# A conditioned transformer block on one core: a new start for the first tile, and new orders of work on every engine

## The reference

```python
def _tc_rmsnorm(x, t, gw, gb, bw, bb):
    g = (t @ gw.T + gb)[:, None, :]
    b = (t @ bw.T + bb)[:, None, :]
    inv_rms = jax.lax.rsqrt(jnp.mean(x * x, axis=-1, keepdims=True) + EPS)
    return g * x * inv_rms + b

x1 = x + _attention(_tc_rmsnorm(x, t, g1w, g1b, b1w, b1b), Wq, Wk, Wv, Wo)   # 16 heads of 16
block = x1 + _swiglu(_tc_rmsnorm(x1, t, g2w, g2b, b2w, b2b), gate_w, hid_w, out_w)   # hidden 1024
return x + block
```

## Time and profile before

| | |
|---|---|
| median of three runs (lowest, highest) | 959.45 us (959.16, 959.62) |
| the profiled execution: time, span on the core | 959.58 us, 957.5 us |
| busy: PE, PEld | 908.0 us (95%), 773.5 us (81%) |
| busy: DVE, ACT, POOL | 664.8 us (69%), 559.4 us (58%), 451.9 us (47%) |
| mean granted TensorE clock | 0.986 |
| chain that ended last | PE 82%, ACT 6%, issue 5%, DVE 3%, POOL 2% |

### The profile page before, as it was taken

The page is one execution under the profiler, slowest core; times in us unless marked ns, Lnnn a source line. Parts: engine busy times, 40 slices in busy tenths (PEclk is TensorE's granted clock), DMA queues, the critical chain, the costliest instruction groups (busy, mean ns, idle before and its releaser), DMA issues.

```text
span 957.5 us, 24194 instructions
## 1 busy us (share of the span) xinstructions
PE 908.0 (95%) x8988; PEld 773.5 (81%) x8988; DVE 664.8 (69%) x1082; ACT 559.4 (58%) x1255; POOL 451.9 (47%) x394
## 2 busy tenths in 40 slices
PE   5678999999999999999999999999999999999998
PEld 4466888878888887888888888888888888788887
DVE  3647768576875857778586877858687685868652
ACT  4556656656665666656566655655666566565542
POOL 4454525354463545436354543535455354544433
PEclk9779999999999999999999999999999999999999
DMA  5300101010110101011010111101010010200000
GB/s 191 98 26 23 34 25 56 1 55 22 44 33 22 39 16 55 22 44 33 7 47 22 44 32 44 33 0 55 22 44 33 23 53 0 55 0 1 24 23 23
DMA packets 25595, 34.06 MB, mean 36 GB/s; under 512 B 3296, under 2 KB 20896, under 8 KB 25440
## 3 DMA queue, kind: packets, MB, share of 16 engines
q1 hardware_dynamic: 25344, 33.59, 11.2%
q10 hardware_dynamic: 224, 0.10, 0.0%
HBM read 25.27 MB, written 8.42 MB: 35 GB/s over the span
## 4 chain that ended last, share of the span: by engine, by line
PE 82%; ACT 6%; issue 5%; DVE 3%; POOL 2%; DMA 1%; ACTq 1%; DVEq 0%; SPq 0%; POOLq 0%
PE ps L1082 8%; PE ps L1084 7%; PE ps L1083 7%; PE ps L1221 7%; PE ps L1237 6%; PE ps L1193 6%; PE ps L1227 6%; PE ps L1222 6%; PE ps L1240 6%; PE ps L1238 6%; PE ps L1183 4%; PE ps L1110 4%; PE ps L1208 4%; PE ps L1111 3%; PE ps L1113 3%
## 5 line engine op out<-in xcount | busy, mean ns | idle before, releaser
L284 POOL TENSOR_TENSOR h_lo<-h,h_hi 128x512 fp32r<-128x512 f32 x128 | 165.7, 1295 | 142.4 <-ACT h_hi L511 142.4
L290 POOL TENSOR_TENSOR probs<-probs,recip 128x512 f32<-128x512 f32 x128 | 134.5, 1058 | 105.6 <-DVE recip L825 105.5
L1082 PE MATMUL ps<-out_w_hi,h_hi 128*128 128x256 f32 x512 | 147.2, 287 | 0.7
L1084 PE MATMUL ps<-out_w_hi,h_lo 128*128 128x256 f32 x512 | 144.4, 282 | 0.0
L1083 PE MATMUL ps<-out_w_lo,h_hi 128*128 128x256 f32 x512 | 144.1, 281 | 0.0
L506 ACT ACTIVATE shared<-ps 128x512 f32<-128x512 f32 x128 | 76.1, 595 | 99.7 <-PE ps L1227 99.4
L836 DVE SCALAR_TENSOR_TENSOR shared<-shared,ps 128x512 f32<-128x512 f32 x128 | 87.4, 683 | 46.4 <-ACT shared L506 44.9
L516 ACT ACTIVATE probs<-probs 128x512 f32<-128x512 f32 x128 | 80.7, 631 | 62.5 <-DVE probs L813 61.9
L1221 PE MATMUL ps<-xn_hi,gate_w_hi 128*128 128x512 f32 x256 | 110.2, 430 | 0.4 <-DVE shared L836 0.2
L843 DVE SCALAR_TENSOR_TENSOR h<-shared,ps 128x512 f32<-128x512 f32 x128 | 87.4, 683 | 30.1 <-PE ps L1240 28.7
L1237 PE MATMUL ps<-xn_hi,hid_w_hi 128*128 128x512 f32 x256 | 105.1, 410 | 0.0
(11 more groups left out here) (92 smaller groups left out, 2016.6 us busy)
## 6 DMA issues: line engine op xcount, KB each, us to landing
x_in<-in_x SPq DMA_DIRECT2D x16, 512.0 KB, 3.4
xT_in<-in_xT SPq DMA_DIRECT2D x16, 512.0 KB, 3.2
out<-result SPq DMA_DIRECT2D x15, 512.0 KB, 3.0
inv_all<-inv_rows SPq DMA_DIRECT2D x15, 256.0 KB, 3.8
shared<-in_attT SPq DMA_DIRECT2D x1, 1024.0 KB, 7.8
shared<-in_gateT SPq DMA_DIRECT2D x1, 1024.0 KB, 9.7
shared<-in_hidT SPq DMA_DIRECT2D x1, 1024.0 KB, 5.0
shared<-in_outT SPq DMA_DIRECT2D x1, 1024.0 KB, 5.7
```

The source lines that it names most:

```text
L284: nc.gpsimd.tensor_tensor(h_lo[:, j % KEPT, :], h[:, j % 2, :], h_hi[:, j % KEPT, :].bitcast(F32), ALU.subtract).then_inc(h_lo_done, 1)
L290: nc.gpsimd.tensor_tensor(own, own, recip[:, p % TOGETHER, :].unsqueeze(2).to_broadcast([P, SEQS, L]), ALU.mult).then_inc(divided, 1)
L1082: nc.tensor.matmul(dst, a_hi, b_hi, start=first, stop=False, skip_group_check=skip)
L1084: return nc.tensor.matmul(dst, a_lo, b_hi, start=False, stop=last, skip_group_check=skip)
```

## The change

Semaphores of keys and queries are renamed for the half that they tell of (`keys0_done`, `keys1_done`, `queries0_done`, `queries1_done`), whichever engine makes it.

The start: TensorE spreads the factors ahead of both modulations. VectorE scales into two banks of PSUM, applies gain and shift to both halves there itself (`whole_norm1`) and leaves the result in `xn1`; ScalarE's `second_norm1(0)` goes. ScalarE rounds the weights of values and output after the norm, not before.

The first tile: the copies go crosswise. ScalarE copies both halves of the keys and the second queries, VectorE the first queries. The casts and low parts of gate, hid and out weights move to other places in the lists.

Other tiles: the scores wait for the values of both engines alone, and steps change places in `steady_tile`, `last_tile` and `after_last` on all four engines. No step of these is added or dropped.

```diff
@@ GpSimd
             def first_tile(t, ahead):
-                low_hid_weights()
+                low_gate_weights()
                 divide(t, 0)
+                next_inverse(t)
                 divide(t, 1)
-                next_inverse(t)
                 divide(t, 2)
...
                 divide(t, 7)
+                low_hid_weights()
                 low_norm1(t + 1, 0)
                 low_norm1(t + 1, 1)
                 low_out_weights()
@@ ScalarE
             squares1(0)
...
+            high_att_weights(0)
             for c in range(CH):
                 high_norm1(0, c)
-            high_weights(1, gate_w_in, 16, gate_w_hi[:, :, :].rearrange("p c n -> p (c n)"), 1)
-            first_keys(0)
-            first_queries(0)
+            high_att_weights(1)
...
             def first_tile(t, ahead):
+                high_gate_weights()
+                first_keys(t)
+                keep_input(t)
+                other_keys(t)
+                exp(t, 0)
+                other_queries(t)
+                exp(t, 1)
                 high_hid_weights()
-                keep_input(t)
                 first_values(0)
-                exp(t, 0)
-                exp(t, 1)
+                exp(t, 2)
+                keep_transposed(t, 0)
                 squares1(t + 1)
...
@@ VectorE
                 if alone(u):
                     dve.wait_ge(inv1_mm, 1)
                     factors = ps[:, PAIR, :].rearrange("p (k q) -> p k q", k=BLK)
+                    scaled = ps[:, PAIR + 2:PAIR + 4, :]
...
+            def whole_norm1():
+                for c in range(CH):
+                    scaled = ps[:, PAIR + 2 + c, :].rearrange("p (b q) -> p b q", q=L)
+                    last = nc.vector.tensor_tensor(scaled, scaled, of_sequences(0, c, 0), ALU.mult)
+                last.then_inc(gained1, 1)
+                dve.wait_ge(gained1, 1)
+                for c in range(CH):
+                    nc.vector.tensor_tensor(xn1[:, c, :].rearrange("p (b q) -> p b q", q=L),
+                                            ps[:, PAIR + 2 + c, :].rearrange("p (b q) -> p b q", q=L),
+                                            of_sequences(1, c, 0), ALU.add).then_inc((xn1_first, xn1_second)[c], 1)
...
             def first_tile(t, ahead):
+                first_queries(t)
                 row_maxima(t, 0)
-                second_keys(0)
                 row_maxima(t, 1)
+                row_maxima(t, 2)
                 shift(t, 0)
...
             def steady_tile(t, finish, ahead):
...
                 low_attention(t, 1)
                 second_queries(t + 1)
+                silu(u, 7)
+                hidden(u, 7)
                 first_residual(t)
+                second_keys(t + 1)
                 scale_second_rest(t)
                 first_norm2(t)
                 second_values(t + 1)
@@ TensorE
                 elif r == 0:
-                    pe.wait_ge(k_act_done, t + 1)
-                    pe.wait_ge(k_dve_done, t + 1)
-                    pe.wait_ge(q_act_done, t + 1)
-                    pe.wait_ge(q_dve_done, t + 1)
+                    pe.wait_ge(v_dve_done, t + 1)
                     pe.wait_ge(v_act_done, t + 1)
-                    pe.wait_ge(v_dve_done, t + 1)
-                    pe.wait_ge(x1_done, 2 * t)
...
+            pe.wait_ge(consts_in, 16)
+            spread_factors()
             pe.wait_ge(mod_in, 2 * 16)
             gains_and_shifts(0)
-            pe.wait_ge(consts_in, 16)
-            spread_factors()
             gains_and_shifts(1)
...
             def first_tile(t, ahead):
                 project_k(0, 1)
                 scores(t, 0)
+                project_v(0, 1)
                 project_q(0, 1)
-                project_v(0, 1)
                 project_v(0, 0)
+                transpose_probs(t, 0)
                 scores(t, 1)
-                transpose_probs(t, 0)
...
             def steady_tile(t, finish, ahead):
...
                 hid(u, 1)
+                transpose_probs(t, 0)
+                gate(u, 2)
                 down(u, 0)
-                gate(u, 2)
                 hid(u, 2)
-                transpose_probs(t, 0)
...
                 values_probs(t, 1)
                 project_q(t + 1, 1)
-                project_k(t + 1, 0)
+                hid(u, 7)
                 project_out(t, ahead)
-                down(u, 5)
-                hid(u, 7)
                 project_k(t + 1, 1)
                 project_v(t + 1, 1)
+                down(u, 5)
                 transpose_norm2(t, 0)
                 transpose_norm2(t, 1)
                 project_v(t + 1, 0)
```

More of the change, by code:

```diff
@@ L485, in first_keys @@
                                                 scale=head_mask[:, head:head + 1])
-                last.then_inc(k_act_done, 1)
+                last.then_inc(keys0_done, 1)
             def first_queries(u):
                 act.wait_ge(q_mm, CH * u + 1)
-                nc.scalar.copy(queries[:, 0, :], ps[:, q_bank(u, 0), :]).then_inc(q_act_done, 1)
+                nc.scalar.copy(queries[:, 0, :], ps[:, q_bank(u, 0), :]).then_inc(queries0_done, 1)
             def first_values(u):
@@ L934, in first_tile, with steady_tile, last_tile @@
                 scale_second_rest(t)
+                second_values(t + 1)
+                first_norm2(t)
+            def steady_tile(t, finish, ahead):
+                u = t - 1
+                low_norm2(u)
+                results(t - 2)
+                row_maxima(t, 0)
+                shift(t, 0)
+                silu(u, 0)
+                hidden(u, 0)
+                reciprocals(t, 0)
+                row_maxima(t, 1)
+                silu(u, 1)
+                shift(t, 1)
+                row_maxima(t, 2)
+                hidden(u, 1)
+                reciprocals(t, 1)
+                silu(u, 2)
+                row_maxima(t, 3)
+                shift(t, 2)
+                shift(t, 3)
+                hidden(u, 2)
+                reciprocals(t, 2)
+                silu(u, 3)
+                reciprocals(t, 3)
+                hidden(u, 3)
+                silu(u, 4)
+                hidden(u, 4)
+                row_maxima(t, 4)
+                row_maxima(t, 5)
+                shift(t, 4)
+                low_attention(t, 0)
+                shift(t, 5)
+                scale_rows(t + 1)
+                reciprocals(t, 4)
+                reciprocals(t, 5)
+                first_norm1(t + 1)
+                silu(u, 5)
+                row_maxima(t, 6)
+                hidden(u, 5)
+                shift(t, 6)
+                row_maxima(t, 7)
+                shift(t, 7)
+                reciprocals(t, 6)
+                reciprocals(t, 7)
+                silu(u, 6)
+                hidden(u, 6)
+                low_attention(t, 1)
+                second_queries(t + 1)
+                silu(u, 7)
+                hidden(u, 7)
+                first_residual(t)
+                second_keys(t + 1)
+                scale_second_rest(t)
                 first_norm2(t)
                 second_values(t + 1)
-            def steady_tile(t, finish, ahead):
+            def last_tile(t, finish, ahead):
                 u = t - 1
@@ L1372, in last_tile @@
                 hid(u, 1)
+                down(u, 0)
                 transpose_probs(t, 0)
@@ L1377, in last_tile @@
                 gate(u, 3)
-                hid(u, 3)
                 transpose_probs(t, 2)
                 transpose_probs(t, 3)
+                hid(u, 3)
+                scores(t, 1)
                 gate(u, 4)
-                scores(t, 1)
+                down(u, 1)
                 hid(u, 4)
-                down(u, 0)
-                down(u, 1)
-                gate(u, 5)
                 values_probs(t, 0)
                 transpose_probs(t, 4)
+                gate(u, 5)
                 down(u, 2)
+                transpose_probs(t, 5)
                 hid(u, 5)
                 gate(u, 6)
-                transpose_probs(t, 5)
                 transpose_probs(t, 6)
@@ L1396, in last_tile @@
                 values_probs(t, 1)
+                gate(u, 7)
+                project_out(t, ahead)
+                hid(u, 7)
                 down(u, 3)
-                project_out(t, ahead)
-                gate(u, 7)
-                hid(u, 7)
                 down(u, 4)
@@ L1424, in after_last @@
                 hid(u, 5, False)
+                down(u, 2)
                 gate(u, 6)
```

277 lines of the change are left out of this document (118 added, 159 removed).

## The result

The kernel after takes 954.69 us (median of five runs, 952.91 to 955.30) against 959.62 us before (five runs beside it): a ratio of 0.994, 95% interval 0.9924 to 0.9955. So it is faster by 4.9 us, about half a percent, where I forecast 14.9; the interval lies clear of 1. Its profiled execution took 954.4 us, with a span of 952.4 us (957.5 before).

| stretch | before | after | difference | forecast |
|---|---|---|---|---|
| start to scores of tile 1 | 79.64 | 73.53 | −6.1 | −6.5 |
| tile 1 | 57.45 | 58.20 | +0.75 | −0.3 |
| tiles 2 to 14, 13 x | 56.45 | 56.20 | −3.2 | −7.2 |
| scores of tile 15 to the end | 86.62 | 90.05 | +3.4 | −0.9 |

A forecast was written before the change was run, and what follows sets the result against it. TensorE was taken to bound the loop, a chain through all engines the first tile. First tile −6.5, tile 1 −0.3, thirteen loop tiles −7.2 and the end −0.9 make −14.9: from 959.58 to 944.7 us, range 938 to 955.

The forecast's parts named there:

- The first tile: From the start to the scores of tile 1: a shorter chain through all engines, −6.5 us (bounds −3 and −9).
- the rows speak for PSUM as the reason: Norm at the start: gain and shift out of PSUM take 0.65 us each, against 1.93 and 2.73 beside GpSimd.
- The faster products: Start: without TensorE's wait, products run at the higher clock sooner; 1.6 us taken back (bounds 0 and 2.4).
- the hidden weights' low part: First tile: moved behind divide 7 on GpSimd, 4.6 us ahead of xn1_lo; projections start at 53.7 to 54.5.
- The waits: Ahead of each tile's scores: seven waits become two, −0.27 us per tile.
- The orders of the loop: Loop tiles: new step orders give −0.28 us per tile, mostly from down 0 finding its low part ready.
- Elsewhere I find no product later than its inputs: Loop: apart from down 0 no product waits for inputs; tightest are transpose 0 (0.1 to 0.25 us ahead) and transpose 3.
- The end: Last tile: −0.6 us at the norm's transposes and −0.3 from waits, −0.9 us in all (bounds 0 and −1.3).
- The last part trades one early stall for another: nothing: The last part, at the kernel's end: one early stall replaces another, no change in time.
- Tile 1: The tile after the first, with a slow clock at its start in either kernel: −0.3 us.
- Rival (d): Tile's end: second keys' copy delays VectorE's scaling of the second residual, 1.2 us lost per tile; 966 us, chance 0.08.
- Rival (a): Loop: the orders give nothing and only the shorter wait works; 948.7 us, chance 0.17.

## Why the prediction was right and wrong

- **The first tile: right in sum, and partly for the wrong reason.** The scaling came at 9.13 (I said 9.1), two gains or two shifts took 1.3 (0.65 each), the scaling for tile 1 began at 42.98 (near 44), the projections of tile 1 began at 54.67 (53.7 to 54.5), the scores at 73.53 (73.1). But "the rows speak for PSUM as the reason" gave the place too much: it is worth 1.0 of 3.8 us. (My upper end, "20.1, that is as late as before", compared the norm's end with that of xn_lo; the norm ended at 18.11.) The faster products gave back 2.2 us where I took 1.6: from the projections to the first scores it takes 4.49 us (16.45 to 20.94) for 6.73 (20.23 to 26.96). And I priced the hidden weights' low part as a step in series on GpSimd. In fact VectorE's add was held until it ended, and the casts came behind that. The two ways happen to end at nearly the same time, so the number was right by luck; an earlier place takes 3.4 us off.
- **The waits: right.** −0.27 forecast, −0.22 measured alone. But the sum has one seam too many: of the fifteen, one stands in the first tile's 6.5 us, one in tile 1 and thirteen in the loop, and "−0.3 from the waits" in the last tile has none left.
- **The orders of the loop: the step that failed.** I took −0.28, as "the chain transposes, norm, casts, values is the same length". Its steps are the same, but not what runs beside them: the scaling took 1.0 us more beside a low part, and TensorE lost 0.73 us of it. I had the price before me, for I took just that for the late step in the last tile, and I didn't ask in the loop what GpSimd would do when its input came earlier. ScalarE's cast of chunk 7 moved ahead of the squares, and so GpSimd's low part became ready before the inverse behind which it was listed. The orders' own gain was mis-sized too: 0.76 us, not 0.28. I looked for idle time, "at most about 13 us in the loop", and found one late product, down 0. "Elsewhere I find no product later than its inputs" was wrong: a projection and a hid waited in each tile as well, in time that the profile counts as TensorE's busy time, out of which 9.4 us came.
- **VectorE beside GpSimd.** The Trainium skill, page "SBUF — State Buffer", section "Who interferes with whom", says that a VectorE instruction in a two-port mode, as `tensor_scalar` can be, contends with GpSimd, and one with two SBUF inputs with GpSimd's reads of SBUF, and that whichever starts first holds up the other for the whole of its instruction. The runs agree: two scalings took 0.61 us alone and 1.63 when GpSimd's 1.28 us began 0.07 us ahead; an add took 0.69 alone and 4.87 behind the start of 4.94.
- **The end: wrong.** −0.6 for the stall at the transposes was right, the stall is gone. For a new stall within the last tile I had no term; the nearest, "The last part trades one early stall for another: nothing", failed. The stall is 2.85 us of standing at the values' products, and the lower clock behind that. With the 0.69 us won at the transposes, the stretch still lost 3.4 us. I hadn't followed VectorE's new list in the last tile to the bank that hid and attention share.
- **Tile 1: wrong in sign.** I put in −0.3, with a slow clock "at its start in either kernel". It is at the lower level behind the scores of tile 1 until about 83 us before (granted clock 0.51 from 80 to 82, 0.64 from 82 to 84), some 3.4 us, and from 73.53 to about 78 after (0.50 from 74 to 78, 0.97 from 78 to 80), some 4.5, behind a stand of 4.73 us instead of 3.51; tile 1 took 0.75 us more. The run with filling products puts the clock's whole price in that tile at 2.1 us (57.67 to 55.59).
- **The rivals.** The measured time lies at the upper end of the range, and came by none of the rivals as written. Rival (d) named the place, the gap ahead of the norm's transposes, but its mechanism, the second keys, cost nothing. Rival (a) gave the right size for the loop: the orders came to nothing, but as a gain of 0.76 and a loss of 0.73 us per tile.

## What to carry to other kernels

When a step becomes ready earlier, look at what it then runs beside: here a cast that ScalarE made earlier moved a step of GpSimd onto one of VectorE's. Put GpSimd's long SBUF work where VectorE reads PSUM or stands still, and read the duration of a VectorE instruction, not only its start, in every stretch that a new order touches. Follow the queue of each engine to the buffers that two stages share, and follow the last tile as carefully as the loop: it has its own lists, and here they cost 3.4 us. Look for late inputs among the waits of TensorE's weight loads too, since its busy time can hide them.

## What the runs showed of the hardware that I had not expected

A VectorE instruction of 0.69 us was held for the rest of a GpSimd instruction of 4.94 us (46.50 to 51.37 beside 45.88 to 50.82): not slowed by a share, but held until about its end. It goes the other way too: GpSimd's division, 1.04 us at its shortest, took 2.78 us when it started 0.16 us behind VectorE's scaling of 2.03 us (43.14 behind 42.98, in the kernel after). And TensorE's busy time isn't a fixed sum of products: the same 7280 took 712.3, 721.7 or 725.7 us at a granted clock of 1.00, by the lists of all engines, and short waits for inputs are counted in it.
